# Three gate and up products of the first batch in the last pair's step, and the last stage's weights laid out and loaded anew

## The reference

```
xn    = layernorm(x)
qu, ku, vu, qc, kc, vc = split(xn @ W_qkv.T)          # 6 x 512 columns
term1 = lower_triangle((qc/8) @ vu.T)
look  = strict_upper_triangle(sigmoid((qu/8) @ ku.T))
Su    = term1 @ look.T
attn  = softmax(causal((qc/8) @ kc.T - silu(Su)))
a     = concat_heads(attn @ vc) @ W_out.T
h     = silu(xn @ wg.T) * (xn @ wu.T)                 # 768 hidden, integer weights / 127
out   = x + a + h @ wd.T
```

## Time and profile before

| | us |
|---|---|
| median of 3 runs | 1125.51 |
| profiled execution, whole | 1131.08 |
| its span, first to last instruction | 1129.4 |
| TensorE matmul busy | 1096.2 (97%) |
| VectorE, ScalarE, GpSimd busy | 830.7, 751.5, 541.5 |
| last pair step begins (TensorE) | 889.91 |
| stage of batch 2 begins | 986.44 |

### The profile page before, as it was taken

One profiled execution on the slowest core, in us unless ns is written; L12 is line 12 of the kernel. 1 busy time (PEld: TensorE's weight loads), 2 busy tenths in 40 slices (PEclk: granted clock), 3 DMA queues, 4 the chain that ended last, 5 costly groups with the idle time before them and its releaser, 6 DMA issues.

```text
span 1129.4 us, 21341 instructions
## 1 busy us (share of the span) xinstructions
PE 1096.2 (97%) x7936; PEld 984.5 (87%) x7936; DVE 830.7 (74%) x1705; ACT 751.5 (67%) x1389; POOL 541.5 (48%) x623
## 2 busy tenths in 40 slices
PE   5999999999999999999999999999999987999997
PEld 4889898988898989898988998999899876889997
DVE  5677787778777877787777777777777747577775
ACT  5677777777777777777777777777777744344433
POOL 0365555555555555555555555555555543322130
PEclk9999999999999999999999999999999978999999
DMA  5000211131113111311121113110100623745641
GB/s 186 1 1 19 81 34 34 33 90 34 34 34 90 34 34 34 89 34 34 34 89 34 34 34 90 34 29 20 57 19 20 261 74 114 261 149 191 225 145 58
DMA packets 44249, 81.88 MB, mean 73 GB/s; under 512 B 2928, under 2 KB 23664, under 8 KB 41584
## 3 DMA queue, kind: packets, MB, share of 16 engines
q1 hardware_dynamic: 44144, 80.49, 22.8%
HBM read 45.35 MB, written 35.13 MB: 71 GB/s over the span
## 4 chain that ended last, share of the span: by engine, by line
PE 92%; DVE 3%; ACT 2%; DMA 1%; issue 1%; POOL 0%; SPq 0%; DVEq 0%; ACTq 0%
PE X L670 23%; PE X L594 20%; PE X L779 7%; PE X L708 7%; PE X L788 7%; PE X L654 6%; PE X L679 6%; PE X L638 5%; PE X L624 5%; PE X L609 4%; DMA v_s<-heads_out 1%; DVE L_s L1238 1%; PE X L585 1%; ACT prob L945 1%; ACT T_s L923 0%
## 5 line engine op out<-in xcount | busy, mean ns | idle before, releaser
L518 POOL TENSOR_SCALAR prob<-prob,inv 128x512 f32<-128x512 f32 (+3 forms) x256 | 294.7, 1167 | 13.0 <-DVE inv L1197 13.0
L670 PE MATMUL X<-L_s,T_s 128*128 128x128 f32 (+3 forms) x1920 | 284.9, 303 | 3.9 <-issue 2.6
L670 PEld LDWEIGHTS X<-L_s,T_s 128*128 128x128 f32 x1920 | 269.1, 191 | 15.2 <-issue 4.9
L594 PE MATMUL X<-xT,W 128*128 128x512 f32 x960 | 245.5, 402 | 1.4 <-DVE xT L1221 1.4
L594 PEld LDWEIGHTS X<-xT,W 128*128 128x128 f32 x960 | 175.0, 190 | 43.7 <-DVE xT L1221 1.8
L937 ACT ACTIVATE gate<-X 128x1024 f32<-128x1024 f32 (+1 forms) x96 | 84.8, 883 | 162.3 <-PE X L670 162.3
L492 POOL TENSOR_SCALAR_AFFINE_SELECT gate<-gate 128x256 f32<-128x256 f32 (+1 forms) x96 | 47.2, 492 | 268.4 <-DVE gate L1171 268.4
L1171 DVE SCALAR_TENSOR_TENSOR gate<-gate,X 128x1024 f32<-128x1024 f32 (+1 forms) x96 | 99.8, 1040 | 99.5 <-ACT gate L937 99.5
L945 ACT ACTIVATE prob<-prob,least 128x512 f32<-128x512 f32 (+3 forms) x256 | 142.1, 594 | 4.1 <-DVE least L1185 4.1
L1164 DVE TENSOR_TENSOR T_s<-X,T_s 128x1024 fp32r<-128x1024 f32 (+1 forms) x96 | 100.5, 1047 | 40.6 <-ACT T_s L923 40.6
L1157 DVE SCALAR_TENSOR_TENSOR L_s<-tanh_l,L_s 128x1024 fp32r<-128x1024 f32 (+1 forms) x96 | 104.5, 1089 | 27.2 <-ACT L_s L929 27.2
(11 more groups left out here) (83 smaller groups left out, 1859.4 us busy)
## 6 DMA issues: line engine op xcount, KB each, us to landing
heads_out<-o_s SPq DMA_DIRECT2D x64, 256.0 KB, 3.3
xT_copy<-xT SPq DMA_DIRECT2D x8, 1024.0 KB, 7.8
w_split<-w_parts SPq DMA_DIRECT2D x22, 256.0 KB, 4.3
W<-w_split SPq DMA_DIRECT2D x3, 1536.0 KB, 14.7
xb<-in_L_attn_x SPq DMA_DIRECT2D x8, 512.0 KB, 5.8
xT<-xT_copy SPq DMA_DIRECT2D x4, 1024.0 KB, 6.2
tanh_l<-in_L_attn_x SPq DMA_DIRECT2D x8, 512.0 KB, 5.2
gate<-heads_out SPq DMA_DIRECT2D x4, 1024.0 KB, 6.8
```

What stands on the lines that cost most here:

```text
L518: last = pool.tensor_scalar(v, v, inv[:, h, w - 1:w], None, ALU.mult)
L594: last = pe.matmul(out, sh.W[:, a, k, cols], xT[:, c, k, :], start=(n == 0), stop=(n == 3 * KD - 1))
L670: last = pe.matmul(both[:, h, at:at + (J + 1) * P], T_s[:, h, a, to:to + P], L_s[:, h, c, WIDE[J + 1]:WIDE[J + 1] + (J + 1) * P], start=(J ...
```

## The change

Weights: the gate and up weights go to the columns of W that belong to pairs 0 to 2 of the first four projections, down goes over the fifth, and W_out into the fourth quarters that are left. A `project_o` matmul therefore reads its 256 columns of W_out as two pieces of 128. Gate and up are loaded in step 30 by 8 DMAs with rows of 1.5 KB. Down and out are loaded in step 31 by 8 DMAs, with rows of 3 KB and of 512 bytes. The products m = 0 to 2 of batch 0 stand in step 31, in banks of the table. The flag is read, and the branch taken, between steps 30 and 31, and both branches hold step 31 and all stages. The first stage has the products 3 to 5, the scores of pair 31, the attention of pair 30 and five `down`. The transposes and the attention of pair 31 move to the second stage. GpSimd adds the heads of batch 0 ahead of its last normalising. The loads of xT of batch 1 and of the heads of batch 1 move forward. The last batch's output is finished and stored in two halves.

```
+    def runs(self, a, k, t, n):
+        return self.W[:, a, k, t * INNER:(t + n) * INNER].rearrange("p (t c) -> p t c", t=n)
+    def gate_w(self, a, k, m):
+        return self.W[:, a, k, m // 3 * INNER + m % 3 * P:m // 3 * INNER + (m % 3 + 1) * P]
+    def up_w(self, a, k, m):
+        return self.gate_w(a, k, m + 6)
+    def down_w(self, a, m):
+        at = 4 * INNER + m % 3 * DIM
+        return self.W[:, a, m // 3, at:at + DIM]
+    def out_w(self, a, m):
+        return self.runs(a, m // 2, 0, 4)[:, 2 * (m % 2):2 * (m % 2) + 2, 3 * P:INNER]
...
-         ("Sc", 1, (0, 1)), ("L", 2, (4, 5)), ("proj", QU, (6,)), ("proj", KU, (7,)), ("Sc", 2, (2, 3)),
-         ("T", 2, (4, 5)), ("proj", VU, (0,)), ("proj", QC, (1,)), ("O", 0, (2, 3)), ("V", 0, (5,)),
-         ("proj", KC, (4,)), ("XT", 0, (2, 3)), ("Su", 0, (6, 7)), ("PT", 0, (0, 1)), ("PT", 1, (4,)),
-         ("Su", 1, (2, 3)), ("PT", 2, (6, 7)), ("Su", 2, (4, 5))]
+         ("Sc", 1, (0, 1)), ("L", 2, (4, 5)), ("proj", QU, (6,)), ("proj", KU, (7,)), ("GU", 0, (6, 7)),
+         ("Sc", 2, (2, 3)), ("T", 2, (4, 5)), ("proj", VU, (0,)), ("proj", QC, (1,)), ("GU", 1, (0, 1)),
+         ("O", 0, (2, 3)), ("V", 0, (5,)), ("proj", KC, (4,)), ("GU", 2, (4, 5)), ("XT", 0, (2, 3)),
+         ("Su", 0, (6, 7)), ("PT", 0, (0, 1)), ("PT", 1, (4,)), ("Su", 1, (2, 3)), ("PT", 2, (6, 7)),
+         ("Su", 2, (4, 5))]
...
+    if kind == "GU":
+        return step == LAST_G
...
+        def act_of(b, m):
+            if b > 0 or m > 3:
+                return act_s[:, m % 2, :]
+            return xb[:, 2 * m:2 * m + 2, :].rearrange("p n d -> p (n d)") if m < 2 else o_s[:, 0, m - 2, :]
         xres = flat_tanh[:, 1024:2048].rearrange("p (n d) -> p n d", n=TT)
-        y_s = flat_prob[:, 0:1024].rearrange("p (n d) -> p n d", n=TT)
+        y_s = xb[:, :, :]
...
-        G, U = [both[:, 0, :] for both in double[0:2]], [both[:, 1, :] for both in double[0:2]]
+        def gate_up_bank(b, m):
+            if b > 0:
+                return double[m % 2]
+            return bank("GU", m) if m < 3 else double[(0, 0, 3)[m - 3]]
+        def o_out(g):
+            if g == LAST_G:
+                return flat_prob[:, 0:1024].rearrange("p (h t) -> p h t", h=2)
+            return o_s[:, g % 2 if g < LAST_G - 1 else 1, :, :]
...
+            if kind == "GU":
+                return hidden_done, n + 1
...
```

SyncE and GpSimd:

```
+                    sp.dma_start(to, o_out(g)[half * DH:(half + 1) * DH, :, :]).then_inc(o_stored[par], 16)
+            def load_gate_up():
+                sp.wait_ge(proj_filled, proj_count(LAST_G - 1, KC))
+                sp.wait_ge(chunk_stored, CHUNKS * 16)
+                for a in range(2):
+                    for n in range(2):
+                        for k in range(KD):
+                            to = sh.runs(a, k, 2 * n, 2)[:, :, 0:3 * P].bitcast(F32)
+                            sp.dma_start(to, w_split[n][:, a, k * HIDDEN:(k + 1) * HIDDEN].rearrange("p (t c) -> p t c", t=2)) \
+                              .then_inc(w_loaded[n], 16)
+            def load_down_out():
+                for k in range(KD):
+                    for a in range(2):
+                        at = k * 3 * DIM
+                        sp.dma_start(sh.W[:, a, k, 4 * INNER:4 * INNER + 3 * DIM].bitcast(F32),
+                                     w_split[2][:, a, at:at + 3 * DIM]).then_inc(w_loaded[2], 16)
+                for k in range(KD):
+                    for a in range(2):
+                        sp.dma_start(sh.runs(a, k, 0, 4)[:, :, 3 * P:INNER].bitcast(F32),
+                                     w_split[3][:, a, k * 512:(k + 1) * 512].rearrange("p (t c) -> p t c", t=4)) \
+                          .then_inc(w_loaded[3], 16)
...
-                    sp.wait_ge(chunk_stored, CHUNKS * 16)
-                    for n in range(4):
-                        sp.dma_start(placed[n].bitcast(F32), w_split[n]).then_inc(w_loaded[n], 16)
+                    load_down_out()
+                if part == LAST and q == 2:
+                    load_gate_up()
                 if back2:
                     store_o(g - 2, q % 2)
...
             sp.wait_ge(scores_emptied, after(LAST_G, 2))
             load_o(0)
-            load_xT(1)
             store_o(LAST_G - 1, 0)
-            store_o(LAST_G, 1)
+            sp.wait_ge(h_low, 4)
+            sp.wait_ge(o_stored[0], 32 * (LAST_G // 2 + 1))
+            load_o(1)
             batches(ffn)
-            store_y(BATCH - 1)
-            sp.wait_ge(y_stored, 16 * BATCH)
+            for i in range(2):
+                sp.wait_ge(y_done, 2 * BATCH - 1 + i)
+                sp.sem_inc(ticks, 1)
+                to = rows(out, BATCH - 1, SEQ).rearrange("(n p) d -> p n d", p=P)
+                sp.dma_start(to[:, 2 * i:2 * i + 2, :], y_s[:, 2 * i:2 * i + 2, :]).then_inc(y_stored, 16)
+            sp.wait_ge(y_stored, 16 * BATCH + 16)
...
+            ffn(0, FIRST)
             for j in range(3):
                 norm(LAST_G, j)
-            batches(ffn)
+            for b in range(1, BATCH):
+                ffn(b, MIDDLE)
...
```

TensorE:

```
+                if part == LAST and q == 3:
+                    gate_up(0, 0, now["products"])
                 if back1:
                     scores(part, b, q, g, 2)
...
+                if part == LAST and q == 3:
+                    gate_up(0, 1, now["products"])
...
+                if part == LAST and q == 3:
+                    gate_up(0, 2, now["products"])
...
+                if b == 0:
+                    both = both or take_bank(LAST, BATCH - 1, LAST_G, "GU", m)
+                    pe.wait_ge(w_loaded[0], 64)
+                    pe.wait_ge(w_loaded[1], 64)
                 else:
+                    both = double[m % 2]
                     pe.wait_ge(hidden_done, b * HT + m - 1)
-                for bank, w in ((G[m % 2], sh.gate_w), (U[m % 2], sh.up_w)):
+                if b == 1 and m == 1:
+                    pe.wait_ge(o_copied, LAST_G)
+                for half, w in enumerate((sh.gate_w, sh.up_w)):
...
-                                         parts[a][:, m, t * P:(t + 1) * P], w[:, c, m, :],
+                                         parts[a][:, m, t * P:(t + 1) * P], w(c, m),
...
-                        pe.wait_ge(PT_low, after(LAST_G, 0))
+                        pe.wait_ge(scores_emptied, after(LAST_G, 2))
+                        pe.wait_ge(w_loaded[2], 64)
                     elif b == 1:
-                        pe.wait_ge(o_copied, LAST_G + 1)
+                        pe.wait_ge(PT_low, after(LAST_G, 2))
...
+                        if b == 2:
+                            pe.wait_ge(o_copied, LAST_G + 1)
...
+            def ffn_first(products):
                 g = LAST_G + 1
+                pe.wait_ge(PT_low, after(LAST_G - 1, 0))
+                gate_up(0, 3, products, double[0])
+                pe.wait_ge(silu_done, after(LAST_G, 1))
+                scores(LAST, BATCH, 0, g, 0, double[1])
+                pe.wait_ge(PT_low, after(LAST_G - 1, 2))
+                scores(LAST, BATCH, 0, g, 1, double[3])
                 pe.wait_ge(silu_done, after(LAST_G, 2))
-                scores(LAST, BATCH, 0, g, 0, double[2])
-                pe.wait_ge(PT_low, after(LAST_G - 1, 0))
-                scores(LAST, BATCH, 0, g, 1, double[0])
-                pe.wait_ge(silu_done, after(LAST_G, 1))
-                scores(LAST, BATCH, 0, g, 2, double[1])
-                pe.wait_ge(PT_low, after(LAST_G - 1, 2))
-                attend(LAST, BATCH, 0, g, double[3])
-            def ffn_first(products):
+                scores(LAST, BATCH, 0, g, 2, double[2])
+                pe.wait_ge(scores_emptied, after(LAST_G, 0))
+                attend(LAST, BATCH, 0, g, double[1])
+                pe.wait_ge(hidden_done, 4)
+                gate_up(0, 4, products, double[0])
+                pe.wait_ge(scores_emptied, after(LAST_G, 1))
+                gate_up(0, 5, products, double[3])
+                for m in range(5):
+                    down(0, m, products)
...
```

```
+                gate_up(1, 0, products)
+                gate_up(1, 1, products)
                 project_o(0, 0)
-                down(0, 2, products)
                 project_o(0, 1)
+                gate_up(1, 2, products)
                 project_o(0, 2)
-                down(0, 3, products)
                 project_o(0, 3)
+                down(0, 5, products)
+                turn_probs(LAST, BATCH, g, 0, double[3])
+                gate_up(1, 3, products)
+                pe.wait_ge(y_done, 2)
+                turn_probs(LAST, BATCH, g, 1, double[2][:, 0, :])
+                pe.wait_ge(PT_low, after(LAST_G, 0))
+                turn_probs(LAST, BATCH, g, 2, double[3])
+                gate_up(1, 4, products)
+                pe.wait_ge(PT_low, after(LAST_G, 1))
+                attend(LAST, BATCH, 1, g + 1, double[2])
+                down(1, 0, products)
+                down(1, 1, products)
+                gate_up(1, 5, products)
```

(112 more changed lines are left out.)

134 lines of the change are left out of this document (49 added, 85 removed).

## The result

The changed kernel takes 1113.53 us (median of 4, 1110.77 to 1113.76), the kernel before beside it 1125.3 (4 runs, 1124.95 to 1125.71): ratio 0.989, 95% interval 0.9873 to 0.9907.

The account below looks back on a forecast made before the run. TensorE bounds the kernel; 25.0 us of idle and slow clock between 889.91 and 986.44 can come back. Stage 2 begins 16.9 earlier, with the end 18.1: 1125.5 - 18.1 = 1107.4 us, range 1101 to 1114.

Parts of the forecast that it names:

- The median is 5.6 lower than the profiled one: Last step: carries this difference from the profiled execution over whole, 1125.5 - 18.1 = 1107.4 us.
- Step 31: Three products fill its idle stretches at full clock; from 889.91 it ends at 917.3, including 0.8 for the branch.
- Weights: Loads of gate and up weights and of batch 0's xT are hidden, costing step 31 nothing.
- First stage: After step 31: products 3 to 5, scores, attention of pair 30, five `down`, from 917.3 to 932.4.
- New wait: Second stage: `project_o(0, 0)` waits 2.3 us for `low_o`, of which 0.4 is GpSimd's adds holding VectorE.
- The rest to stage 2: From the first `project_o`: 28.1 of work, 2.3 of waits and 0.7 of clock, 31.1 us, to 969.5.
- The end: Finishing and storing the last batch in halves saves 0.6 of a sum and 0.6 of the store, 1.2 us.
- The branch shows: Rival, before step 31: branch costs up to 3.8 instead of 0.8, plus 1.7 of clock; 1112.1 us, 12%.
- The products fill nothing: Rival: ScalarE and VectorE set step 31, so products only lengthen it and 8.3 us of gain goes; 1115.7, 5%.
- Two pieces: Rival: `project_o` matmuls reading W_out in two pieces stream slower in all eight stages, up to 1152.7 us; 3%.
- Adds hold VectorE: Rival, ahead of `project_o(0, 0)`: GpSimd's adds hold VectorE their whole length, 4.0 more plus 1.7 of clock; 1113.1, 11%.
- Better cover: Rival: no branch time, no clock drop, adds out of the way, 1.0 less waiting behind; 1104.5 us, 17%.

Follow-up runs that it names:

- experiment 1: The kernel before run and profiled again, unchanged: 1124.96 us (12 runs), ratio 1.0008; its profiled execution took 1122.91.
- experiment 3: GpSimd's adds of the heads replaced by a one-input scaling of the first half: 1124.67 us on the kernel before, 1113.16 us on the changed kernel.
- the repeats: The changed kernel run and profiled again, unchanged, in two sets: 1112.29 us (5 runs) and 1112.91 us (6 runs).
- experiment 4: The kernel before with 5.7 us of unused matmuls added in step 31, where the change puts its products: 1121.47 us, ratio 0.9984.
- experiment 5: The changed kernel with only 2 of 8 matmuls kept in each of step 31's three products, 4.3 us less work: 1114.7 us, ratio 0.9916.
- experiment 8: The changed kernel with GpSimd's last normalising put back ahead of the adds for batch 0: 1117.02 us, ratio 0.9942.
- Experiment 10: The changed kernel with GpSimd normalising first, second-stage queues rewritten to suit, and GpSimd waiting between its adds of batch 0: 1112.41 us, ratio 0.9915.

## Why the prediction was right, and where not

**The step that failed is the last one:** "The median is 5.6 lower than the profiled one, and I carry the difference over whole". It treats the 5.6 as an offset that both kernels have. It was loss of the kind that the change removes. The profiled execution had the 4.4 us hold of `low_h` and the low clock behind it. The traces of before without that hold reach stage 2 in 88.9 and 90.3 us from the start of step 31 (experiments 1 and 3), not in 96.5, and the second of them, at 1124.87, still has the low clock of step 31. So some 6 of the 16.9 us that the forecast brings back there are not lost in executions like those of the median. (The second trace has the adds replaced, so this rests on the one-input operations costing the same as the adds.) The changed kernel shows neither loss: no long hold in its three traces, and no execution of 15 above 1114.4 or with a clock below 0.997. So the gain is 18 against the rare execution (1131.08 - 1113.0), 12 against the frequent ones (1124.9 - 1113.0) and 7 against the best (1120.3 - 1113.0). The forecast for the profiled execution, 1113.0, is the median of the changed kernel's 15.

That the time still fell inside the range is in part luck. The range reached up to 1114 for the branch (1112.1) and for the adds (1113.1), and neither is what happened.

The terms, in the order of the prediction:
- *Step 31*: 27.4 forecast, 26.4 measured. The branch was mis-sized at 0.8 and costs nothing: 888.70 stands 1.49 behind 887.21, and twelve such matmuls took 1.49 in the repeat of the kernel before (887.33 to 888.82). The gap ahead of the sum was 0.59, not 1.0. Clock full, as forecast. The idea that `low_L` is late next held (the releaser is L_s).
- *Weights*: hidden, as forecast. No product waits for W or xT.
- *First stage*, from 915.12 to 930.89: 15.8, forecast 15.1. The first attention waits 0.55 where 0.2 was taken; 0.3 stays unassigned.
- *New wait*: 2.59, forecast 2.3, at the place forecast. The adds held three LOW parts by 0.4 to 0.5 each, as taken. `project_o(0, 0)` came 48.7 behind the start of step 31, forecast 48.5.
- *The rest to stage 2*: 31.2, forecast 31.1, but by other terms. The waits are 0.59 instead of 2.35, and the clock costs 1.6 instead of 0.7: 24 matmuls took 4.44 from start to start (937.37 to 941.81), and at 0.118 each they are 2.8. With the 28.1 of work that is 30.3, so 0.9 stays unassigned. The sum was right by errors of opposite sign.
- *The end*: 1.2 forecast, 2.5 in the first pair of traces (6.1 and 3.6), 1.1 in the repeats (6.6 and 5.5). The sum's 0.6 was wrong: before, the whole sum of 1.29 had already begun at 1122.89, while the last matmul ran, and ended 0.86 behind that; now it ends 0.72 behind. The rest is the store, whose last wait was 3.7 to 4.9 when whole and is 2.0 to 2.1 or 3.8 to 4.0 by halves.

**The rivals.** *The branch shows* is out (0). *The products fill nothing* is out by the gaps, and experiments 4 and 5 show the opposite: work put there is free, and work taken out gains nothing. *Two pieces* is out: twelve such matmuls take 1.42 in both kernels. (The 44 matmuls of the earlier trace rows, read in the prediction as `project_o`, are 36 of `project_o` and 8 of `down`, at the same 0.118.) *Adds hold VectorE* is out for the change as made and shown as real for its neighbour, experiment 8 (4.0 for the hold and 1.7 for the clock forecast; 4.1 measured in all). *Better cover* had the branch and the waits behind the first `project_o` right, but not the adds, which hold three LOW parts, and not the clock: behind a gap of 2.6 it does fall.

**The lock on the port.** The trace agrees with the one-instruction lock of the Trainium skill (SBUF — State Buffer, SBUF: two separate sides) where the adds follow a wait: 1.1 to 1.7 for a LOW part, the rest of one add. It does not in three traces where four adds follow the normalising at once (5.12, 3.52, 4.37). Experiment 10 shows that a wait between the adds restores the short hold. The repeat of the kernel before and experiment 4 have the same queue and holds of 1.60 and 1.61, with 0.11 and 0.23 between the normalising's end and the adds. But in the changed kernel the adds of batch 1 follow the normalising at once (948.04), and the `low_h` beside them takes 0.78 (at 951.60). So the missing pause alone does not make the hold. What decides in such a queue stays open.

## What to carry to other kernels

Profile the kernel before twice, or hold its one trace against the spread of its times, before a difference to the median is carried over: where idle stretches trigger a slower clock, the loss varies from execution to execution, and a change that fills them removes the variation as well as the mean. Idle stretches of TensorE that another chain sets are room for work: 5.7 us of matmuls went into them for 1.2 at most, and taking 4.3 us out gained nothing. When a wait moves, look at the order on GpSimd before TensorE's: one moved line there was worth 4 us, and moving TensorE's products alone lost 2.
